# The last layer's adapters: the pair's two gathered by transfers, in place of all eight with a mask

## What is computed

```python
H = jnp.einsum('btd,od->bto', x, W)
xa = jnp.einsum('btd,brd->btr', x, A[adapter_idx])
delta = jnp.einsum('btr,bor->bto', xa, Bm[adapter_idx])
return H + delta * scalings[adapter_idx][:, None, None]
```

## Time and profile before

| | |
|---|---|
| timed runs, median of 3 | 1107.1 us (1106.96 to 1110.6) |
| the profiled execution, span from the first to the last instruction | 1135.0 us |
| TensorE's products, busy | 1048.5 us, 92% |
| DVE, ACT, POOL busy | 660.7, 539.0, 535.0 us |
| mean granted TensorE clock | 0.968 of full speed |
| moved by DMA | 196.16 MB, 95337 packets |

### The profile page before, as it was taken

One profiled execution on the slowest core, in us unless ns is written; L12 is line 12 of the kernel. 1 busy time (PEld: TensorE's weight loads), 2 busy tenths in 40 slices (PEclk: granted clock), 3 DMA queues, 4 the chain that ended last, 5 costly groups with the idle time before them and its releaser, 6 DMA issues.

```text
span 1135.0 us, 23836 instructions
## 1 busy us (share of the span) xinstructions
PE 1048.5 (92%) x6438; PEld 709.2 (62%) x6438; DVE 660.7 (58%) x1928; ACT 539.0 (47%) x1337; POOL 535.0 (47%) x597
## 2 busy tenths in 40 slices
PE   7989999997588999999999999999899998999998
PEld 6767777675355566666556666666565666666665
DVE  5889896667344555555555555555455454555552
ACT  4457776674344444434444444444344444444441
POOL 3555444366555454554454545454354454454400
PEclk9999999999579999999999999999899899999999
DMA  3434443563367666565666666666565565566641
GB/s 130 143 116 149 140 146 115 176 197 119 95 205 208 191 194 200 185 195 168 209 201 187 189 202 187 183 207 207 157 202 187 174 203 189 172 185 181 220 141 59
DMA packets 95337, 196.16 MB, mean 173 GB/s; under 512 B 31346, under 2 KB 40114, under 8 KB 87110
## 3 DMA queue, kind: packets, MB, share of 16 engines
q1 hardware_dynamic: 63942, 149.49, 41.0%
q0 software_dynamic: 30784, 44.16, 14.0%
q10 hardware_dynamic: 576, 2.10, 0.5%
HBM read 195.08 MB, written 33.56 MB: 201 GB/s over the span
## 4 chain that ended last, share of the span: by engine, by line
PE 64%; issue 3%; ACT 3%; another core or an unknown queue 2%; DMA 1%; POOL 1%; DVE 0%; ACTq 0%; POOLq 0%; DVEq 0%
PE bank L93 22%; PE bank L1476 11%; PE bank L1451 9%; PE bank L1430 8%; PE bank L1438 8%; PE bank L1417 4%; ACT PT L1230 2%; PE bank L1407 1%; ACT KT L1230 1%; DMA KV<-kv_scratch,idxs 1%; DMA KV<-in_pool,idxs 1%; POOL KV L1132 0%; POOL KVE L1142 0%; POOL KV L1142 0%
## 5 line engine op out<-in xcount | busy, mean ns | idle before, releaser
L1230 ACT ACTIVATE PT<-bank 112x384 f32<-112x384 f32 x256 | 113.7, 489 | 271.7 <-PE bank L1438 225.3
L1308 DVE CUSTOM_DVE_ANT_0 SM<-bank,FM 128x336 f32<-128x336 f32 x256 | 129.7, 507 | 162.2 <-PE bank L1430 121.4
L1142 POOL DMA_INDIRECT KV<-kv_scratch,idxs x96 | 96.1, 1001 | 128.1 <-DMA KV<-in_pool,idxs 104.9
L1142 POOL DMA_INDIRECT KVE<-kv_scratch,idxs_e x93 | 93.3, 1004 | 124.4 <-DMA KVE<-in_pool,idxs_e 99.9
L1239 ACT ACTIVATE PR<-SM,nb 128x336 f32<-128x336 f32 x256 | 145.5, 574 | 1.9 <-DVE nb L1312 1.7
L1132 POOL DMA_INDIRECT KV<-in_pool,idxs x96 | 95.4, 994 | 76.6 <-PE bank L1451 49.9
L1430 PE MATMUL bank<-KT,QB 64*128 64x336 f32 x512 | 113.2, 521 | 15.2 <-ACT KT L1230 11.6
L1132 POOL DMA_INDIRECT KVE<-in_pool,idxs_e x90 | 89.8, 998 | 73.7 <-PE bank L1451 46.9
L1230 ACT ACTIVATE KT<-bank 128x336 f32<-128x336 f32 x128 | 57.6, 450 | 140.0 <-PE bank L1417 132.5
L1476 PE MATMUL bank<-W,XT 128*64 128x512 f32 x512 | 123.7, 604 | 0.0
L1438 PEld LDWEIGHTS bank<-ident,PR 128*112 128x112 f32 x768 | 84.3, 137 | 48.9 <-issue 48.9
(11 more groups left out here) (195 smaller groups left out, 2167.6 us busy)
## 6 DMA issues: line engine op xcount, KB each, us to landing
W<-in_w SPq DMA_DIRECT2D x64, 1024.0 KB
FM<-mask SPq DMA_DIRECT2D x64, 168.0 KB
X<-in_x SPq DMA_DIRECT2D x32, 256.0 KB
x_scratch<-X SPq DMA_DIRECT2D x32, 256.0 KB
qt_scratch<-QT SPq DMA_DIRECT2D x32, 256.0 KB
QB<-qt_scratch SPq DMA_DIRECT2D x32, 256.0 KB
XB<-x_scratch SPq DMA_DIRECT2D x32, 256.0 KB
BB<-in_b SPq DMA_DIRECT2D x64, 128.0 KB
```

The lines of the kernel that those rows point to most:

```text
L1142: pool.indirect_dma_start(out=KV[k][:, c, :], out_offset=None, in_=kv_d, in_offset=bass.IndirectOffsetOnAxis(ap=idxs[k][:, NCH + c:NCH + c ...
L1230: return nc.scalar.activation(dst, src, ACT.Copy)
L1308: v.tensor_tensor_reduce(out=SM[u % 2][:, :], in0=bank[u % 2][:, 0:SPAN], in1=FM[k][:, :], scale=1.0, scalar=-3e38, op0=ALU.add, op1=ALU.m ...
```

## The change

For each pair SP now gathers the two adapters of its sequences into tiles of their own, the A part from SBUF and the B part from a copy in DRAM. In the first part A^T is laid out by adapter and split into AS; B^T is scaled first (`scale_b`), then split into BSH and BSL, which are stored to DRAM before the first body. The mask is now one fixed tile, `amask`, which keeps the rows of each sequence's own adapter. Of `adapter`'s output rows 0 to 31 are high(A) x, rows 32 to 63 low(A) x. XA has four groups of 32 rows: the high part of either, the low part of the first, and the high part of the first again; BG has high B, three times, and low B. So one product sums what were three.

The value loads and all ten transfers are issued by SP between the output store and the wait for x2.

```diff
+                def scale_b():
+                    dve.wait_ge(s_wlate, 16 * 6)
+                    v.tensor_scalar(b_raw, b_raw, scal[:, 0:1], None, ALU.mult).then_inc(s_bsc, 1)
...
+                def adapter_low():
+                    dve.wait_ge(s_wlh, 5)
+                    split(AS[:, :, 0, :], AS[:, :, 1, :], a_raw.rearrange("p (e r) -> p e r", r=RANK))
+                    split(BSH[:, :], BSL[:, :], b_raw).then_inc(s_wl, 1)
...
+            AG = sbt("AG", [P, KC * 2, 2, RANK], F32R)
+            BG = sbt("BG", [P, D], F32R)
+            XAM = sbt("XAM", [2 * 2 * RANK, P])
+            XA = sbt("XA", [P, P], F32R)
...
+                for h, tile in enumerate((BSH, BSL)):
+                    sp.dma_start(bs_d[h].rearrange("e r n -> (e r) n"), tile[:, :].bitcast(F32)).then_inc(s_bso, 16)
...
+                    def adapters(q):
+
+                        numbers = [sp.value_load(aid[0:1, bass.ds(q * 2 + b, 1)], min_val=0, max_val=NA - 1)
+                                   for b in range(2)]
+                        wait(sp, s_xa, q)
+                        for b, e in enumerate(numbers):
+                            sp.dma_start(AG[:, :, b, :].bitcast(F32),
+                                         AS[:, :, :, :].rearrange("p (e k) h r -> p e (k h) r", e=NA)[:, bass.ds(e, 1)]
+                                         .bitcast(F32)).then_inc(s_ag, 16)
+                        wait(sp, s_l3, q)
+                        for s in range(4):
+                            for b, e in enumerate(numbers):
+                                row = 32 * s + RANK * b
+                                sp.dma_start(BG[row:row + RANK, :].bitcast(F32), bs_d[s // 3, bass.ds(e, 1)]
+                                             ).then_inc(s_bg, 16)
...
                     if adapted:
                         store(p - 2)
+                    if dense:
+                        if isinstance(p, int) and p == 1:
+                            sp.wait_ge(s_bso, 32)
+                        adapters(p - 1)
...
                     if adapted:
                         dve.wait_ge(s_xa, at(r, 1, 0))
-                        v.tensor_tensor(XAM[:, :, :], bank[1 if last_dense(p) else 7][:, 0:P].rearrange("p (b t) -> p b t", b=2),
-                                        adapt[:, bass.ds(r * 2, 2)].unsqueeze(2).to_broadcast([P, 2, T]),
+                        two = 2 * RANK
+                        wait(dve, s_l3, r)
+                        v.tensor_tensor(XAM[:, :], bank[1 if last_dense(p) else 7][0:2 * two, 0:P], amask[:, :],
                                         ALU.mult).then_inc(s_xam, 1)
-                        xam = XAM[:, :, :].rearrange("p b t -> p (b t)")
                         dve.wait_ge(s_xam, at(r, 1, 0))
-                        v.tensor_copy(XAH[:, :], xam).then_inc(s_xah, 1)
+                        v.tensor_copy(XA[0:2 * two, :], XAM[:, :]).then_inc(s_xah, 1)
+                        v.tensor_copy(XA[3 * two:4 * two, :], XAM[0:two, :])
                         dve.wait_ge(s_xah, at(r, 1, 0))
-                        low(XAL[:, :], xam, XAH[:, :]).then_inc(s_xal, 1)
+                        low(XA[2 * two:3 * two, :], XAM[0:two, :], XA[0:two, :]).then_inc(s_xal, 1)
...
                 def adapter(r, of):
                     pe.wait_ge(s_xt3, at(r, 1, 0))
-                    exact_products(mm, bank[of][:, 0:P], [(a_h[:, k, :], a_l[:, k, :], *x3t[k]) for k in range(KC)],
-                                   True, True).then_inc(s_xa, 1)
+                    pe.wait_ge(s_ag, at(r, 32, 31))
+                    for k in range(KC):
+                        high_low = AG[:, 2 * k:2 * k + 2, :, :].rearrange("p h b r -> p (h b r)")
+                        for i, part in enumerate(x3t[k]):
+                            last = mm(bank[of][0:4 * RANK, 0:P], high_low, part, start=k == 0 and i == 0,
+                                      stop=k == KC - 1 and i == 1)
+                    last.then_inc(s_xa, 1)
 
                 def adapted_sum(r, of):
                     pe.wait_ge(s_xal, at(r, 1, 0))
-                    exact_products(mm, bank[of][:, :], [(XAH[:, :], XAL[:, :], b_h[:, 0, :], b_l[:, 0, :])],
-                                   False, True).then_inc(s_l3, 1)
+                    pe.wait_ge(s_bg, at(r, 128, 127))
+                    mm(bank[of][:, :], XA[:, :], BG[:, :], start=False, stop=True).then_inc(s_l3, 1)
```

More of the change, by code:

```diff
@@ L134, in build @@
         QT = sb("QT", [P, 2, KC, T])
-        NWL = KC * D * 2 + KC * P + D
+        NWL = KC * D * 2
+        NWR = NWL + KC * P + D
         wlh = sb("wlh", [P, NWL], F32R)
         wll = sb("wll", [P, NWL], F32R)
+        AS = sb("AS", [P, NA * KC, 2, RANK], F32R)
+        BSH = sb("BSH", [P, D], F32R)
+        BSL = sb("BSL", [P, D], F32R)
         def late(tile, which):
-            a, n = {"wo": (0, D), "w3": (KC * D, D), "a": (2 * KC * D, P), "b": (2 * KC * D + KC * P, D)}[which]
-            k = 1 if which == "b" else KC
-            return tile[:, a:a + k * n].rearrange("p (k n) -> p k n", k=k)
+            a = {"wo": 0, "w3": KC * D}[which]
+            return tile[:, a:a + KC * D].rearrange("p (k n) -> p k n", k=KC)
         s_const = sem("const_ready")
@@ L635, in _ @@
                 between.update({21: go_on(1), 23: go_on(2), 26: go_on(4)})
-                between.update({27: late_low(0), 28: late_low(1), 29: late_low(2),
-                                31: in_turn(late_low(3), late_low(4))})
+                between.update({27: late_low(0), 28: in_turn(scale_b, late_low(1)), 29: late_low(2),
+                                31: in_turn(late_low(3), adapter_low)})
                 bodies(dve, body, between)
@@ L727, in _ @@
                     24: late_weights((late(wlr, "w3"), t["w3T"].rearrange("(k p) n -> p k n", p=P))),
[L728 to L729 removed]
+                    25: late_weights((a_raw, t["aT"]), (b_raw, t["bT"]))})
                 store_qt(PAIRS - 1)
@@ L857, in late_high, with adapter_high @@
                     return run
+                def adapter_high():
+                    act.wait_ge(s_bsc, 1)
+                    copy(AS[:, :, 0, :], a_raw.rearrange("p (e r) -> p e r", r=RANK))
+                    copy(BSH[:, :], b_raw).then_inc(s_wlh, 1)
                 bq = bank[2][:, :].rearrange("p (h d) -> p h d", h=H)
@@ L907, in _ @@
                 bodies(act, body, {6: lambda: sines(2, EARLY, PAIRS)} |
-                       {26: in_turn(late_high(0), late_high(1))} | {p: late_high(p - 25) for p in (27, 28, 29)})
+                       {26: in_turn(late_high(0), late_high(1)), 27: late_high(2), 28: late_high(3), 29: adapter_high})
             @block.tensor
@@ L1080, in build @@
             s_xt3 = sem("x3t_ready")
+            s_bso = sem("b_stored")
+            s_ag = sem("a_gathered")
+            s_bg = sem("b_gathered")
             s_xa = sem("xa_done")
@@ L1402, in _ @@
                 wo_h, wo_l, w3_h, w3_l = late(wlh, "wo"), late(wll, "wo"), late(wlh, "w3"), late(wll, "w3")
-                a_h, a_l, b_h, b_l = late(wlh, "a"), late(wll, "a"), late(wlh, "b"), late(wll, "b")
                 def turn_x(tile, s_done):
```

34 lines of the change are left out of this document (17 added, 17 removed).

## The result

| kernel | median, us | lowest and highest | ratio, 95% interval |
|---|---|---|---|
| before | 1107.03 | 1106.87 to 1110.6 | |
| changed | 1163.59 | 1161.62 to 1166.73 | 1.0515, 1.0497 to 1.0534 |
| changed, measured again (e10) | 1169.63 | 1164.56 to 1171.21 | 1.0580, 1.0555 to 1.0605 |

The change costs 56.5 us. I had forecast 1090. The kernel before took 1105 to 1108 us beside e9 to e18, but 1130.9 beside e1 to e4 and 1142.5 beside e5 to e8, on other chips, so a ratio of e1 to e8 is compared with those of e9 to e18 only with reserve, and the kernels of e1 and e8 were run again as e15 and e16.

What follows compares the result with a forecast made beforehand. TensorE was taken to bound the kernel: 1.26 us saved a pair less 0.70 us of late QB is 0.56 us over 31 bodies, 17 us off the 1107.1 median, giving 1090 us; full range 1064 to 1142.

Steps and rivals of the forecast that it cites:

- QB late by 0.7 us a body: PE waits for QB at `scores`: 0.4 us in the clean body, 1.0 in the mean one, 0.7 taken.
- SP's sum of 7.9 us: Issue time added to SP between output store and XB1: value loads 1.4, A's gathers 1.6, B loads 4.9 us.
- A's gathers: Two gathers on SP, 1024 pieces of 64 bytes each: 0.8 us each, 1.6 together; bounds 0.5 and 1.7 each.
- The eight B loads: Eight loads of B rows on SP, 0.61 us each as for `bd`: 4.9 us, bounds 3.8 and 5.8.
- TensorE saves 1.26 us a pair, all on the chain: On TensorE, `adapter` saves 0.80 us and `adapted_sum` 0.46; bounds 0.90 and 1.26, all on the chain.
- QB late from a sum of 7.2 on: On SP's queue, nothing is late with a sum below 7.2 us; QB's landing was taken as 2.7 us.
- Rival 2: SP's queue becomes the bound, PE waiting for QB at `scores(pr, 0)`: slower, 1139 at a sum of 9.5; chance 0.36.
- Other work at nothing: Added DMA traffic, hidden by POOL's gathers running about a body ahead, and first-part changes like `scale_b`: costed at nothing.
- The rule that spoke against the change: One large transfer for many small: ten in turn on SP take 20 us, over 300 us for the kernel; no chance.
- the case that I called the likeliest: QB on SP's queue partly late, kernel faster: 1075 to 1101 us; chance 0.27.
- The bounds of S, 6.2 to 10.6: Low and high bounds, in us, of the issue time added to SP's queue, around the 7.9 taken.
- the point of decision at 8.5: Sum of SP's added issue time, about 8.5 us (7.2 + 1.26), from which rival 2 decides.

Runs made afterwards that it cites:

- e9: Kernel before with TensorE's part alone: adapter as 8 products of 64 columns, one product by B, low-part products left out; 1100.11 us, ratio 0.9954.
- e18: e14's kernel with A's gather as one 1 KB piece per partition (256 pieces a pair instead of 1024) and 16 products of 64 columns; 1113.77 us, 1.0079.
- e1: Changed kernel with the eight B loads moved behind the queries and window masks of the next pair; ratio 1.0551.
- e4: Changed kernel with one B load of 64 rows per adapter (2 in place of 8) and A gathered in 128 columns; ratio 1.0394.
- e5: e1's kernel with A gathered once, early, instead of for each pair (products use wrong adapters); ratio 1.0279.
- e8: Kernel before plus, per pair, two value loads and eight B loads into a tile nothing reads, no gather of A; ratio 1.0076.
- e15: e1's kernel run again; 1154.40 us, ratio 1.0436.
- e16: e8's kernel run again; 1111.96 us, ratio 1.0036.
- e17: e9's kernel plus e16's value loads and eight B loads between output store and XB1, low-part products still left out; 1088.18 us, ratio 0.9844.
- e13: Changed kernel with SP's order turned: the adapters' value loads and ten transfers go ahead of the first expert load, W(0); 1118.48 us, ratio 1.0100.
- e12: Changed kernel with 16 products of the identity ahead of `scores(pr, 0)`; 1174.73 us, ratio 1.0629.
- e14: e4's kernel with the adapters' value loads and transfers put ahead of W(0), as in e13; 1115.25 us, ratio 1.0064.
- e7: Kernel before plus, per pair, two value loads and the two gathers of A into a tile nothing reads, no B loads; ratio 1.0024.
- e11: e4's kernel with ten products of the identity behind the adapter; 1159.73 us, ratio 1.0494.
- e3: Kernel before plus, per pair, two value loads and ten transfers of the change's shapes into tiles nothing reads; ratio 1.0599.

## Why the prediction was wrong

The forecast had QB late by 0.7 us a body and 1.26 us saved beside it. PE waits 86.2 / 32 = 2.7 us a body for QB: the 2.0 more make 62 of the 73.6 us between 1090 and 1163.6. The step that failed is the sum behind that 0.7, above all what A's two gathers cost SP; with it failed "all on the chain", the worth of what TensorE saves.

- **SP's sum of 7.9 us.** Measured 9.3 in the body shown, 9.5 in the mean. The value loads were right (1.6 us with the gaps against 1.4). A's gathers were sized at 1.6 us; they cost 3.9, above even my upper bound of 3.4. Their own issues take 1.53, but the load behind them stands 2.44 us instead of some 0.4. The row had it: the load behind A^T took 0.69 instead of 0.33. I took that for "a queue effect" and went to the low end. The eight B loads were sized at 4.9 from two `bd` loads in 1.21 us; by themselves they take 3.7 (e16), so this error hid a part of the other. An issue's time is not a property of its own transfer alone: what was issued just before belongs to it.
- **TensorE saves 1.26 us a pair, all on the chain.** The size was right: 0.54 us for the adapter, as by the row of `values` (not the 0.45 of the estimate beside it), and one product of B. Its worth was not. The chain of one body shows what ended last, not how close the next loop is, nor how that loop answers. Alone the saving brought 0.16 us a body (e9, 5 us for 39), and 0.56 with eight loads more on SP (e17). I had written that the gathers "run about a body ahead and hide that"; `landed` makes SP wait for them, and in e9 and e13 they are the loop that bounds.
- **QB late from a sum of 7.2 on.** For the changed kernel this held: 9.5 - 7.2 = 2.3 us late against 2.7 measured, and in e16 and e17, with 5.4 in the bodies shown, PE waits 0.1 and 0.5 us a body (2.1 and 13.2 over some 28). The 2.7 us for QB's landing was right there too (2.8). It is not a rule for other orders: in e9 and e13, with nothing of the adapters ahead of QB, PE waits 0.8 and 1.4 us a body, and QB takes 6.8 us to land in e9.
- **Rival 2's price.** The place and the cause are rival 2's, and so is its sum of 9.5, for which it gave 1139: 24.6 us too few. 2.7 us late less 1.26, over 31 bodies, makes 45 of the 56.5 us lost, and these 45 contain the first bodies (17.8 of the 86.2 us lie before 400 us). The rest agrees with TensorE's busy time: the same 6246 products keep it busy for 1022 us in the changed kernel and 1007 in e9, with a mean granted clock in 400:1100 of 0.96 and 0.98. What the lower clock costs in time stays open, as e12 can't tell it.
- **Other work at nothing.** Once SP's order is out of the way, 1.0% stays in e13 where TensorE's part alone gives -0.5%. In between lie the traffic (POOL waits 250 us for its gathers instead of 230) and the rewritten steps on VectorE; no run separates these two.
- **The rule that spoke against the change.** I gave the rule of the Trainium skill (DMA: Bandwidth & Descriptors, Rules for kernel authors), one large transfer for many small ones, no chance of its own. With six fewer transfers e14 is 0.4 points better than e13, but the two intervals touch, and e14 also moves more of A and has wider products: the rule may point the right way here, and it is worth little beside the order. The Trainium skill (DMA: Bandwidth & Descriptors, Specifications) asks for transfers of at least 512 bytes for full rate; e18 against e14 (pieces of 1 KB against 256 bytes) shows no gain from it here. The 2.0 us that I took from the Trainium skill (DMA: Bandwidth & Descriptors, Anatomy of one DMA) is given there for transfers issued by GpSimd; SP's B loads landed after a median of 2.6 us (e10) and overlapped, as the rows of `bd` had it.

Rival 2 had 0.36, more than the case that I called the likeliest (0.27). The bounds of S, 6.2 to 10.6, lie evenly around the point of decision at 8.5, so they didn't decide; the reading of one row did. And the two sides were not alike: I had checked what TensorE's saving could hit next on ACT and DVE, and gave the loop of gathers one sentence.

Left open: how much of e15 is A's alone. The one run of A alone (e7) was made on the kernel before; TensorE's part with A and without B was not tried. A kernel with the whole change that beats the one before was not found; e14 comes nearest. e17, which does, leaves products out.

## What to carry to other kernels

Before a saving on the bounding engine is counted, ask how long the next loop is, and close it: follow the chain from a transfer's landing through the buffer it frees back to its issue. Its length isn't fixed either: here the gathers took 60 us more of POOL's time once TensorE was quicker. A queue that waits for data in one place of its loop and is urgent in another has its slack in the first place alone; put added transfers ahead of that wait, not behind it (here 5.8% against 1.0% for the same ten transfers). Size an issue by rows with the same neighbours, not by the same form alone. And measure a filler before reading a result by it: these took 1.8 times what I had put them at, and became the bound.

## What was not expected of the hardware

- **More work on a queue made the kernel faster.** e17 has eight loads more than e9 and is 1.1 points faster (0.984 against 0.995, each beside its own kernel before). In e9 XB1, QB and masks are issued right behind W(0), and POOL waits 230 us for gathers (201 in e17). The further behind W(0) QB is issued, the sooner it lands: issued 1.7 us behind it lands after 6.8 us (e9), at 7.8 after 5.2 (e15), at 7.0 and 7.2 after 5.1 and 4.1 (e17, e16), at 10.8 after 2.8 (the changed kernel). That the loads' delay clears the gathers' way is the likely cause; no run moves QB alone. The Trainium skill (DMA: Bandwidth & Descriptors, SWDGE vs HWDGE vs iDMA) says that transfers of GpSimd and of SyncE lie in different queues of the same 16 engines, which take turns between them. The traces fit that, without showing the turns: in e9 one gather lands after 6.84 us, the next after 3.19.
- **Many small pieces delay the issue behind them, not their own.** Two gathers of 1024 pieces of 64 bytes each issue in 1.53 us; the plain load behind them took 3.40 us (e15; 0.36 to 3.75 in 30 bodies). In the body shown of e13, where SP waits between A's gathers and the B loads, the eight loads take 3.72 us, as without A. With half the pieces, of 256 bytes each, the delay is hardly there: in e11 the two gathers issue in 1.52 us and the two B loads behind them in 1.28.
- **Results that seem to come later than the matmul records end.** Beside the slower kernels before, ScalarE and VectorE stood in front of results of TensorE whose records had long ended, with no releaser that the profile names ("remote"), and then the clock fell. In e5 (PE's `scores` and `turn`, then VectorE on the first's result, then ScalarE on the second's):

```profile
842.43 0.83 PE L1482 MATMUL bank<-KT,QB 64*128 64x336 f32 x4 [0.18 <-ACT KT L1282]
...
843.19 0.87 PE L1490 MATMUL bank<-ident,PR 128*112 128x128 f32 x6
...
845.28 0.51 DVE L1360 CUSTOM_DVE_ANT_0 SM<-bank,FM 128x336 f32<-128x336 f32 x1 [1.65 <-remote]
...
849.67 0.87 ACT L1282 ACTIVATE PT<-bank 112x384 f32<-112x384 f32 x2 [5.46 <-remote]
```

The granted clock was 1.00 until 848 us and 0.50, the level of 1.2 GHz, from 850 to 856 us; TensorE had been idle from 846.3 to 850.7, and the DMA engines busy at 0.89 to 0.99 from 842 on. ScalarE has 97.8 us of such waits in 400:1100 of e5, 20 in the profile of the kernel before, whose span of 1135.0 is 27.9 us above its median, 2.7 in e3, and none in the changed kernel or in e9 to e18. No profile of the kernel before was taken beside e1 to e8, so that these waits are what made it slower there is not shown. What holds the results back no run shows.
